# Transformer layer with 32-head cross attention: scores by row quadrants in place of a block-diagonal query tile

## What is computed

```
q = rope(layernorm(x) @ Wq, pos)            # 32 heads of 8 numbers
k, v = split(ctx @ Wkv);  k = rope(k, pos)
w = softmax(q @ k.T / sqrt(8))              # for each head, 128 x 128
x = x + (w @ v) @ Wout + bout
h = clip(round(relu(quant(layernorm(x)) @ quant(W1).T + b1) / s2), 0, 15) * s2    # 1024 wide
x = x + h @ quant(W2).T + b2
```

## Time and profile before

| what | us |
|---|---|
| median of 3 runs | 290.56 (288.91 to 291.06) |
| the profiled execution, its own time | 288.7 |
| span of its trace, first to last instruction | 286.9 |
| busy: TensorE | 249.2 (87%) |
| busy: VectorE | 223.0 (78%) |
| busy: ScalarE | 200.0 (70%) |
| busy: GpSimd | 128.2 (45%) |

### The profile page before, as it was taken

The page is one execution under the profiler, slowest core; times in us unless marked ns, Lnnn a source line. Parts: engine busy times, 40 slices in busy tenths (PEclk is TensorE's granted clock), DMA queues, the critical chain, the costliest instruction groups (busy, mean ns, idle before and its releaser), DMA issues.

```text
span 286.9 us, 8646 instructions
## 1 busy us (share of the span) xinstructions
PE 249.2 (87%) x2786; PEld 181.8 (63%) x2786; DVE 223.0 (78%) x569; ACT 200.0 (70%) x440; POOL 128.2 (45%) x265
## 2 busy tenths in 40 slices
PE   0055749999999999999999999999999999999663
PEld 0044538667677777777777777777777767656441
DVE  2979977978889787978898889888889777884431
ACT  3213526776797969797979797979797978778413
POOL 7727485453717272626262636363636260420110
PEclk9999786999999999999999999999999999999855
DMA  8951214421212131213121312131212111200101
GB/s 153 329 133 37 47 39 93 142 48 40 49 40 49 40 85 40 50 40 83 38 47 38 83 38 47 38 83 38 47 38 77 40 40 41 74 3 5 37 0 37
DMA packets 31786, 17.39 MB, mean 61 GB/s; under 512 B 6545, under 2 KB 31377, under 8 KB 31761
## 3 DMA queue, kind: packets, MB, share of 16 engines
q1 hardware_dynamic: 29696, 17.06, 24.1%
q10 hardware_dynamic: 2064, 0.02, 0.4%
HBM read 6.31 MB, written 2.10 MB: 29 GB/s over the span
## 4 chain that ended last, share of the span: by engine, by line
PE 71%; DVE 10%; issue 7%; POOL 6%; ACT 5%; ACTq 0%; POOLq 0%; DVEq 0%
PE ps_misc L962 36%; PE ps_av L962 13%; PE ps_max L962 13%; PE ps_exp L962 9%; DVE red L681 2%; ACT h_i L622 2%; POOL v_strip L490 1%; DVE xn L858 1%; POOL q_rows L473 1%; DVE by_sin L792 1%; DVE by_cos L787 1%; POOL q_diag L442 1%; POOL q_rows L431 1%; DVE xn L763 1%; POOL k_rows L432 1%
## 5 line engine op out<-in xcount | busy, mean ns | idle before, releaser
L801 DVE TENSOR_REDUCE mx<-ps_max 128x4 f32<-128x512 f32 x128 | 87.5, 687 | 23.8 <-PE ps_max L962 21.3
L593 ACT ACTIVATE expo<-ps_exp 128x512 f32<-128x512 f32 x128 | 77.7, 607 | 18.9 <-PE ps_exp L962 17.3
L962 PE MATMUL ps_exp<-q_diag,k_stack 128*128 128x512 f32 x128 | 60.3, 471 | 0.0
L962 PE MATMUL ps_max<-k_stack,q_diag 96*128 96x128 bf16 (+1 forms) x512 | 53.0, 226 | 1.3 <-DVE mx L801 1.2
L962 PE MATMUL ps_av<-expo,v_strip 128*32 128x128 f32 x1024 | 54.1, 285 | 0.0
L622 ACT ACTIVATE h_i<-ps_misc,b1q,relu_scale 128x128 int16<-128x128 f32 x128 | 48.5, 473 | 2.5 <-PE ps_misc L962 2.5
L962 PEld LDWEIGHTS ps_max<-k_stack,q_diag 96*128 96x128 bf16 (+1 forms) x512 | 30.9, 99 | 25.1 <-issue 23.5
L490 POOL TENSOR_TENSOR v_strip<-v_comp,zeros 128x32 f32<-128x32 f32 x128 | 27.9, 255 | 19.7 <-PE ps_av L962 19.7
L962 PEld LDWEIGHTS ps_av<-expo,v_strip 128*32 128x32 f32 x1024 | 20.3, 108 | 21.8 <-issue 14.6
L473 POOL TENSOR_TENSOR q_rows<-rot,q_rows 128x256 f32<-128x256 f32 x16 | 12.2, 764 | 38.6 <-ACT q_rows L568 38.6
L587 ACT CAST k_stack<-ps_misc 128x512 fp32r<-128x512 f32 x32 | 18.9, 591 | 11.0 <-PE ps_misc L962 5.8
(11 more groups left out here) (123 smaller groups left out, 500.2 us busy)
## 6 DMA issues: line engine op xcount, KB each, us to landing
q_diag<-q_comp SPq DMA_DIRECT2D x128, 64.0 KB, 2.1
w<-in_L_ffn_W_dram SPq DMA_DIRECT2D x2, 1024.0 KB, 8.7
out_dram<-y SPq DMA_DIRECT2D x8, 256.0 KB, 2.2
c_in<-in_ctx_dram SPq DMA_DIRECT2D x16, 64.0 KB, 2.1
x_all<-in_x_dram SPq DMA_DIRECT2D x1, 1024.0 KB, 6.0
x_all<-in_x_dram SPq DMA_DIRECT2D x1, 512.0 KB, 5.5
q_diag<-mxT SPq DMA_DIRECT2D x32, 8.0 KB, 1.8
x_all<-in_x_dram SPq DMA_DIRECT2D x2, 128.0 KB, 2.8
```

What stands on the lines that cost most here:

```text
L593: act.activation(expo[:, g % EXPO, :], ps_exp[g % 2][:, :], ACT.Exp, scale=SCALE).then_inc(exp_done, 1)
L801: dve.tensor_reduce(out=mx[:, r, 4 * g:4 * g + 4], in_=ps_max[g % 2][:, :].rearrange("p (h k) -> p h k", h=4), axis=AX.X, op=ALU.max).then ...
L962: return pe.matmul(out, lhsT, rhs, start=start, stop=stop, skip_group_check=True, **kw)
```

## The change

- `PARTS` is 24. The maximum's row is row 24 of each head's own 32 partitions (`NEG_ROW`), not one row for the group. `q_comp`, `q_diag`, `place_queries`, `clear_diagonal` are gone; `copy_queries` writes `q_stack` itself. `q_stack` and `k_stack` have three buffers.
- The eight groups are four units of eight heads. `scores_for_max` and `scores_for_exp` issue eight matmuls of 128 columns a unit, each on a head's own 32 partitions, alternating between two quadrants and between the two banks of `ps_max` or `ps_exp`. The host permutes the columns of Wq and Wk to suit.
- `maxima` and `exponentials` take both banks in one instruction (128 x 1024), four a step each. As both banks are one buffer now, the matmuls of unit u wait for the reader of unit u - 1.
- `weigh_values` does two groups at once, one unit behind; `expo` has three buffers of 1024.
- The order of the pieces and the places (g) of the other stages' work change on TensorE and ScalarE. On VectorE all but `maxima` keep their places.
- The hardware loop is gone: all 22 steps are written out, and waits have constant values.

```diff
-LOOP_FROM, LOOP_TO = S_FFN + 2, BATCH
-XT, SQ0, MX1, QK, SQ1, XQ, AT1, H0, SK0, MX0, AT2, VV, H1, WO, SK1, YY = range(16)
+XT, MX1, SQ0, QK, AT1, SQ1, XQ, SK0, H0, MX0, AT2, VV, H1, WO, SK1, YY = range(16)
 PIECE_BANK = (1, 2, 0, 1, 2, 0, 1, 0, 2, 1, 0, 2, 1, 0, 2, 0)
-EXPO = 4
-LAG = 2
+UNITS = 4
+EXPO = 3
-NEG_ROW = 96 + 3 * HD
+PARTS = 3 * HD
+NEG_ROW = PARTS
+STACK = 3
...
-        ps_max = [bank("ps_max0"), bank("ps_max1")]
-        ps_exp = [bank("ps_exp0"), bank("ps_exp1")]
+        ps_max = stack.enter_context(nc.psum_tensor("ps_max", [128, 2, 512], F32))
+        ps_exp = stack.enter_context(nc.psum_tensor("ps_exp", [128, 2, 512], F32))
...
# ScalarE
-                act.copy(q_comp[:, r, 4 * half:4 * half + 4, :], src).then_inc(q_ready, 1)
+                act.copy(q_stack[:, at, 4 * half:4 * half + 4, :], src).then_inc(q_ready, 1)
...
-            def exponentials(st, g):
-                st.wait(act, exp_scores, S_ATT, GROUPS, g + 1)
-                st.wait(act, av_done, S_ATT, GROUPS, g + 1 - EXPO)
-                act.activation(expo[:, g % EXPO, :], ps_exp[g % 2][:, :], ACT.Exp, scale=SCALE).then_inc(exp_done, 1)
+            def exponentials(st, u):
+                st.wait(act, exp_scores, S_ATT, UNITS, u + 1)
+                st.wait(act, av_done, S_ATT, GROUPS, 2 * (u - EXPO) + 2)
+                at = (UNITS * st.batch(S_ATT) + u) % EXPO
+                act.activation(expo[:, at, :], ps_exp[:, :, :].rearrange("p m t -> p (m t)"), ACT.Exp, scale=SCALE)\
+                    .then_inc(exp_done, 1)
...
-                    if g == 4 and st.has(S_STACK):
+                    if g == 5 and st.has(S_STACK):
                         copy_keys(st, 0)
                     if g == 5 and st.has(S_OUT):
                         copy_attnT(st)
...
-                    if g == 3 and st.has(S_FFN):
+                    if g == 5 and st.has(S_FFN):
                         relu(st, 0)
-                    if g == 5 and st.has(S_PROJ):
+                    if g == 6 and st.has(S_PROJ):
                         copy_v(st)
-                    if g == 5 and st.has(S_FFN):
+                    if g == 7 and st.has(S_FFN):
                         relu(st, 1)
                     if g in (6, 7) and st.has(S_PROJ):
                         split_high(st, g - 6)
...
# VectorE
-                dve.tensor_reduce(out=mx[:, r, 4 * g:4 * g + 4],
-                                  in_=ps_max[g % 2][:, :].rearrange("p (h k) -> p h k", h=4),
+                dve.tensor_reduce(out=mx[:, r, 8 * u:8 * u + 8],
+                                  in_=ps_max[:, :, :].rearrange("p m (i k) -> p (m i) k", i=4),
                                   axis=AX.X, op=ALU.max).then_inc(max_done, 1)
...
-                    if st.has(S_MAX):
-                        maxima(st, g)
+                    if g % 2 == 0 and st.has(S_MAX):
+                        maxima(st, g // 2)
...
# TensorE
+            def unit_heads(u):
+                half, pair = u // 2, u % 2
+                return [(m, i, slice(32 * (2 * pair + m), 32 * (2 * pair + m) + 32), 4 * half + i)
+                        for i in range(4) for m in range(2)]
+            def scores_for_max(st, u):
+                at = st.ring(S_MAX, STACK)
+                if u % 2 == 0:
+                    st.wait(pe, q_ready, S_MAX, 2, u // 2 + 1)
+                    st.wait(pe, k_ready, S_MAX, 2, u // 2 + 1)
+                st.wait(pe, max_done, S_MAX, UNITS, u)
+                for m, i, rows, g in unit_heads(u):
+                    rows = slice(rows.start, rows.start + PARTS)
+                    ins = mm(ps_max[:, m, 128 * i:128 * i + 128], top_halves(q_stack[rows, at, g, :]),
+                             top_halves(k_stack[rows, at, g, :]))
+                ins.then_inc(max_scores, 1)
...
-                st.wait(pe, exp_done, S_ATT, GROUPS, g - 1)
-                mm(ps_exp[g % 2][:, :], k_stack[:, r, g, :], q_diag[:, r, g, :]).then_inc(exp_scores, 1)
+                st.wait(pe, exp_done, S_ATT, UNITS, u)
+                for m, i, rows, g in unit_heads(u):
+                    rows = slice(rows.start, rows.start + NEG_ROW + 1)
+                    ins = mm(ps_exp[:, m, 128 * i:128 * i + 128], k_stack[rows, at, g, :], q_stack[rows, at, g, :])
+                ins.then_inc(exp_scores, 1)
...
                 for g in range(GROUPS):
+                    u = g // 2
+                    if g % 2 == 0:
+                        if st.has(S_MAX):
+                            scores_for_max(st, u)
+                        if st.has(S_ATT):
+                            scores_for_exp(st, u)
+                        if u == 0 and st.has(S_OUT):
+                            weigh_values(st, UNITS - 1, S_OUT)
+                        if u > 0 and st.has(S_ATT):
+                            weigh_values(st, u - 1, S_ATT)
```

296 lines of the change are left out of this document (117 added, 179 removed).

## The result

The changed kernel takes 363.45 us (median of 4 runs, 362.15 to 364.83), the kernel before 289.89 (288.91 to 291.06). The ratio is 1.254, with a 95% interval of 1.246 to 1.261: slower by a quarter. The forecast was 338, its range 318 to 374.

What follows compares the result with a forecast made beforehand. TensorE, never idle in full steps, bounds the kernel at 14.45 us a step; 13.0 of own work plus 5.6 of waits makes 18.6. 288.7 + 46 + 3 + 1 - 3 = 336, with 1.9 more 338; range 318 to 374.

Steps and rivals of the forecast that it cites:

- the rival of the quadrants: Score matmuls in different quadrants don't run beside each other: +2.9 on 12 steps, about 373 us; chance 0.16.
- the rival of the clock: TensorE's clock halves for some 1.3 us of work after each wait for relu(0): +14, 352 us; chance 0.12.
- TensorE's own work 14.45 to 13.0: Us per full step: 0.37 saved on tiling changes, 0.94 on maxima, 0.13 on exponentials' scores.
- The four waits, 5.6: Late waits of TensorE in each full step, which add: 1.94, 0.37, 2.2 and 1.1 us.
- waits 1 and 3: Unit 2's scores wait for rope and unit 1's reduction, 1.94 us; the value projection waits for relu(0), 2.2 us.
- 2 and 4: AT2 waits behind copy_keys(0), 0.37 us; project_y waits behind relu(1), 1.1 us.
- The steps 6 to 16, +46: Eleven full steps at 18.6 us against 14.45, +4.2 each.
- The start-up, -3 and +3: Zeroing of q_diag goes, -3 us; in steps 3 to 5 one wait stands against the saving, +1 each, +3.
- wait 1: Unit 2's scores wait because VectorE reduces unit 1 only after rope: 1.94 us a full step, longer in steps 3 to 5.
- The last steps, +1: Steps 17 to 21: the saving on scores about given back by relu(1) standing later, +1 us.
- The loop, nothing: Writing out the hardware loop gains nothing, as TensorE has no idle time from its registers.
- Hidden and faster: Rival: waits are hidden and the saving of 1.44 a step stands, 270 us; chance 0.06.

Runs made afterwards that it cites:

- e4: The changed kernel's products, maxima and exponentials with new orders for TensorE, ScalarE, VectorE and the banks of pieces: 278.37 us, ratio to before 0.961 to 0.973.
- e1: The changed kernel with matmuls that nobody reads filling TensorE's four late waits of each full step: 336.64 us.
- e2: The changed kernel with ScalarE's first relu moved ahead of the copy of the attention's transposed rows: 350.94 us.
- e5: The changed kernel with VectorE's rotation moved behind the reduction of unit 1's maxima: 342.46 us.
- e6: The changed kernel with 30 unread matmuls in only one late wait, the one before the value projection: 349.18 us.
- e12: The changed kernel with the moves of e2 and e5, and unread matmuls in the three waits left: 310.72 us.
- e9: The kernel before with only its hardware loop written out: 289.27 us against 289.38, ratio 0.9996.
- e7: e4 with both heads of each pair read from the same quadrant, number and sizes of products kept: 343.54 us.
- e8: e4 with 219 unread matmuls in TensorE's waits of the first steps: 268.98 us, ratio to before 0.929 to 0.936.
- e11: e8 with the maxima's products on the two quadrants the exponentials' products leave free, both kinds issued by turns: 262.96 us, ratio to before 0.904 to 0.912.
- e3: The changed kernel with score products issued quadrant after quadrant instead of by turns, quadrants used unchanged: 368.37 us.

## Why the prediction was right, and where it was off

The direction and the cause were right: slower, by waits in the written order. The time is 25 above the forecast and past the forecast's own bound of 350. It lies inside the range of 318 to 374 only because of the room that was kept for the rival of the quadrants, which did not come true; the rival of the clock, which did, had given 352. That the range holds 363 is therefore partly luck.

- *TensorE's own work 14.45 to 13.0.* Right: 13.20 where nothing waits (e4). Maxima, exponentials' scores, tiling changes and the two long instructions on VectorE and ScalarE had nearly the durations given.
- *The four waits, 5.6.* Right in place, in releaser and nearly in size: 5.3 read at full clock in e1 (1.95, 0.28, 2.03 and 1.02, against 1.94, 0.37, 2.2 and 1.1 forecast), step 18.31 against 18.6. That the order makes them, and not the new products, is shown by e4. That the waits 1 and 3 don't hang together is shown by e2 and e5; 2 and 4 were not taken away one by one.
- *The steps 6 to 16, +46.* At full clock 18.31 - 14.47 = 3.84 each (e1, and the four steps of e6 without a fall), so 42 for eleven. Right as far as the waits go.
- *The clock.* This is the term that failed: the forecast put it at nothing. The rival had the mechanism and the sign, but it stood apart from the forecast at 0.12, and it was sized at 1.3 us of slow work behind each relu, +14. Measured: 2.1 us a step, 21 in the ten steps. Three things were wrong in it. The stretch is not short: the row 193.55 to 203.80 holds 66 matmuls, and six of the ten steps are like it. It doesn't begin behind the relu but before it, behind the waits for the rotation and the reduction. And the argument against it (250 to 266 us of the kernel before had waits and read nine) leant on waits of at most 0.5 us. With new waits of 5 us in every step the lower clock belonged into the forecast itself.
- *The start-up, -3 and +3.* Wrong. Of the -3, 0.5 was there when step 3 began. Step 3 came out 0.5 shorter than before, where +1 was forecast. The steps 4 and 5 cost +14.1, where +1 each was forecast, and step 6 cost +4.1, where +4.2 was. In the steps 4 and 5 the clock is 0.59, against 0.96 and 1.00 before, and the wait for the reduction is up to 2.0 us long; with the rotation moved and at full clock they take 25.0 (e12) against the 24.3 of before. The forecast had called wait 1 longer there, and then priced the step at +1.
- *The last steps, +1.* Measured -1.1.
- *The loop, nothing.* Right (e9).
- *Quadrants not beside each other.* This rival did not come true. Had it been so, it would have cost +2.72 a step (e7), near the 2.9 given.
- *Hidden and faster.* The saving of 1.3 a step is real, but the order as written cannot show it. e4 shows that it can be had: 278, and 263 with the changes of e8 and e11 on top.

Of the 75.6 us between the two executions, 38 are waits less the saving in the ten steps 7 to 16 and 21 the clock there. The other 16 are the 18 of the steps 4 to 6 less the 2 gained at both ends; in the steps 4 to 6 waits and clock were not fully told apart.

## What to carry to other kernels

A change that makes the bound engine's own work smaller is judged by what that engine has to wait for in the new order, bank by bank and relu by relu; here 1.3 us saved a step stood against 5.3 of waits that only came from where instructions were written. If that engine is TensorE and it will wait in every step, price the waits twice: once as they are, and once for the clock that may fall with them, also if each is short (here 0.7 and 0.9 us one behind the other came before every first fall). When a row of products is tested for working side by side, change where they run, not the order in which they are issued.

## What the runs showed that I had not expected

- Products that nobody reads made the kernel 27 us faster (e1), and the start-up of another about 5 (e8): the granted clock was 1.00 in place of 0.78, and 0.95 in place of 0.66.
- The clock fell in six of ten steps whose longest wait was 0.9 us (e6), and stayed at 1.00 with one wait of 0.7 in each step (e12).
- Four products in four quadrants, two bf16 and two fp32r, start within 0.01 us of each other (e11), and four products issued in a row for one quadrant don't keep the four behind them for another from working beside them (e3 with e7).
- In one quadrant alone, a bf16 product with its load costs 0.057 us and an fp32r one 0.11 (e7).
